# Keys of the second attention computed inside the last output product, two output tiles to a PSUM bank, and the bias added to x ahead of the last power

## The reference, cut to what matters

```
x = x + attention0(norm(x), ctx)          # 16 heads of 16, with biases bq, bk, bv, bo
x = x + ffn0(norm(x))                     # fp4-quantised, silu(gate) * up, width 704
x = x + attention1(norm(x), ctx, mask)    # 16 heads of 64: k = ctx @ W_K, v = ctx @ W_V
x = x + ffn1(norm(x))                     # width 1024
# ffn1: h = fix(x @ w1 + b1); h = fix(piecewise-linear gelu(h)); out = fix(h @ w2 + b2)
```

## Time and profile before

| what | value |
|---|---|
| median of 3 runs | 1011.18 us |
| their range | 1006.55 to 1011.65 us |
| the profiled execution | 1006.48 us |
| its span, first to last instruction | 1004.5 us |
| busy: PE, DVE, ACT, POOL | 913.8, 702.4, 599.6, 194.3 us |
| granted clock of PE, mean | 0.987 |
| chain that ended last | PE 55%, DVE 26%, ACT 10% |

### The profile page before, as it was taken

One profiled execution on the slowest core, in us unless ns is written; L12 is line 12 of the kernel. 1 busy time (PEld: TensorE's weight loads), 2 busy tenths in 40 slices (PEclk: granted clock), 3 DMA queues, 4 the chain that ended last, 5 costly groups with the idle time before them and its releaser, 6 DMA issues.

```text
span 1004.5 us, 16041 instructions
## 1 busy us (share of the span) xinstructions
PE 913.8 (91%) x5508; PEld 583.5 (58%) x5508; DVE 702.4 (70%) x2192; ACT 599.6 (60%) x1671; POOL 194.3 (19%) x307
## 2 busy tenths in 40 slices
PE   3888889999979999999979999999998999999985
PEld 1455565667555666566555556566755565656743
DVE  5799682674789786474697978267488978637358
ACT  2688433882679633794458943498166973369442
POOL 2000000782000000375100000078200000037300
PEclk8999999999999999999999999999999999999999
DMA  9400100000000010000000000000000000000000
GB/s 295 171 1 1 27 1 22 1 2 1 1 1 18 6 27 22 1 1 2 0 1 7 17 27 1 22 2 2 1 0 1 17 7 1 0 1 2 1 0 21
DMA packets 14943, 18.33 MB, mean 18 GB/s; under 512 B 3472, under 2 KB 12048, under 8 KB 14864
## 3 DMA queue, kind: packets, MB, share of 16 engines
q1 hardware_dynamic: 12800, 15.53, 4.8%
q10 hardware_dynamic: 2064, 1.78, 0.6%
HBM read 15.21 MB, written 2.10 MB: 17 GB/s over the span
## 4 chain that ended last, share of the span: by engine, by line
PE 55%; DVE 26%; ACT 10%; issue 4%; SPq 2%; DMA 1%; POOL 1%; POOLq 0%; DVEq 0%; ACTq 0%
PE bank L1030 22%; PE bank L1045 9%; PE bank L1216 5%; PE bank L1296 5%; PE bank L1194 4%; PE bank L1136 4%; DVE row_max L833 3%; ACT ring L564 3%; PE bank L1113 2%; ACT ring L504 2%; ACT ring L601 2%; SPq L391 1%; DVE act_s L755 1%; DMA w_s<-w 1%; DVE big_q L800 1%
## 5 line engine op out<-in xcount | busy, mean ns | idle before, releaser
L418 POOL TENSOR_TENSOR rstd<-var_eps,minus_half 128x2 f32<-128x2 f32 x32 | 22.7, 713 | 643.8 <-DVE var_eps L750 643.8
L504 ACT ACTIVATE ring<-bank 128x512 f32<-128x512 f32 x228 | 125.7, 605 | 28.4 <-PE bank L1045 28.3
L429 POOL TENSOR_TENSOR ring<-ring,row_inv 128x256 f32<-128x256 f32 x192 | 111.9, 612 | 98.7 <-DVE row_inv L927 98.7
L1045 PE MATMUL bank<-ident_s,ring 128*128 128x128 f32 x768 | 105.8, 281 | 4.2 <-ACT ring L504 2.6
L1045 PEld LDWEIGHTS bank<-ident_s,ring 128*128 128x128 f32 x768 | 83.7, 142 | 41.9 <-issue 19.2
L601 ACT ACTIVATE ring<-ring,row_max 128x256 f32<-128x256 f32 x192 | 95.4, 501 | 14.2 <-DVE row_max L920 13.8
L1030 PE MATMUL bank<-ctxT_s,wk_s 128*128 128x512 f32 x160 | 82.0, 639 | 19.9 <-DVE wk_s L992 7.2
L564 ACT ACTIVATE ring<-bank,row_max 128x256 f32<-128x256 f32 x192 | 88.3, 494 | 15.6 <-DVE row_max L833 15.5
L833 DVE TENSOR_REDUCE row_max<-bank 128x2 f32<-128x512 f32 x128 | 79.3, 681 | 16.1 <-PE bank L1113 15.4
L920 DVE CUSTOM_DVE_ANT_0 ring<-bank,maskbias 128x256 f32<-128x256 f32 x192 | 69.9, 420 | 19.2 <-issue 19.2
L1030 PE MATMUL bank<-wgu_s,act_s 128*128 128x352 f32 x256 | 78.8, 461 | 2.9 <-ACT act_s L498 2.9
(11 more groups left out here) (159 smaller groups left out, 1662.3 us busy)
## 6 DMA issues: line engine op xcount, KB each, us to landing
ctxT_s<-ctxT SPq DMA_DIRECT2D x4, 512.0 KB, 3.7
x_s<-x SPq DMA_DIRECT2D x4, 512.0 KB, 4.0
w_s<-w SPq DMA_DIRECT2D x2, 1024.0 KB, 15.7
out<-act_s SPq DMA_DIRECT2D x16, 128.0 KB, 1.7
wk_s<-wk SPq DMA_DIRECT2D x1, 1024.0 KB, 12.9
wv_s<-wv SPq DMA_DIRECT2D x1, 1024.0 KB, 13.9
wq_s<-wq SPq DMA_DIRECT2D x1, 1024.0 KB, 16.2
wo_s<-wo SPq DMA_DIRECT2D x1, 1024.0 KB, 18.0
```

The costliest lines, as they stand in the source:

```text
L429: ins = pool.tensor_tensor(probs1[i % PRING1][:, a, :], probs1[i % PRING1][:, a, :], row_inv[:, i, a:a + 1].to_broadcast([P, SEQ]), ALU.mult)
L504: act.activation(probsT[u % TRING][:, :, :].rearrange("p a q -> p (a q)"), psum(at, key)[:], ACT.Copy).then_inc(drain(at, key), 1)
L1045: ins = pe.transpose(psum(at, key)[:, c * SEQ + a * P:c * SEQ + (a + 1) * P], tile[:, a, c * P:(c + 1) * P], ident_s[:])
```

## The change

Four edits go together.

1. The first three key chunks k1(0), k1(1), k1(2) of a crossing move out of rounds 1 to 3 and into the output product. PE's order is now: output chunks 0 to 3, k1(0), chunk 4, k1(1), chunk 5, scores of round 0, chunks 6 and 7, k1(2). ACT drains k1(0) and k1(1) behind the last query drain, and k1(2) between the exponentials of units 1 and 2 of round 0. They go through banks 4, 5 and 5.
2. To free banks 4 and 5, the four output tiles share two banks (6 and 7), two tiles in each, and `output_bias` is two operations of 512 columns in place of four of 256. In a crossing it stands between the normalising of units 1 and 2 instead of ahead of unit 0.
3. k1 is kept in big_v and v1 in big_q, so the lower half of big_v is no longer a gelu buffer: `GELUS` is 4, and `hidden(m)` waits for yT(m - 4). The opening's raw weights and temporaries move from big_v to big_q with it.
4. POOL's `bias_x(g + 1)` stands ahead of the last `ln_power`, right behind the mask conversion.

The opening pass keeps its order; the closing pass gets edits 2 and 3.

```diff
-GELUS = 5
+GELUS = 4
+KEYS_AHEAD = 3
@@ jobs_layer0
     if with_last_layer:
         jobs_last_out(jobs)
+        for m in range(KEYS_AHEAD):
+            jobs.add(("k1", m), 4 + min(m, 1))
@@
-        jobs.add(("k1", r - 1), 7)
+        if not with_last_layer or r > KEYS_AHEAD:
+            jobs.add(("k1", r - 1), 7)
@@ jobs_last_out
-    for t in range(TILES):
-        jobs.add(("o2", t), 4 + t)
+    for h in range(HALVES):
+        jobs.add(("o2", h), 6 + h)
@@
-        q1, k1, c1 = big_k, big_q, big_c
-        v1 = big_v[:, :, :].rearrange("p (t n) c -> p t (n c)", t=TILES)
+        q1, k1, c1 = big_k, big_v, big_c
+        v1 = big_q[:, :, :].rearrange("p (t n) c -> p t (n c)", t=TILES)
-        gelu_buf = [... ((big_v, 0), (big_v, 1), (big_c, 0), (big_c, 1), (ring, 0))]
+        gelu_buf = [... ((big_v, 1), (big_c, 0), (big_c, 1), (ring, 0))]
@@ gpsimd
                 mask_to_bias()
+                bias_x(g + 1)
                 ln_power(g * 4 + 4)
-                bias_x(g + 1)
@@ scalar, last_layer
+                if with_layer0:
+                    for m in range(KEYS_AHEAD - 1):
+                        layer1_key(at, m)
@@ scalar, layer0_heads
-                        layer1_key(at, r - 1)
+                        if with_weights or r > KEYS_AHEAD:
+                            layer1_key(at, r - 1)
...
                         for i in round_units0(r):
+                            if r == 0 and i == 2 and not with_weights:
+                                layer1_key(at, KEYS_AHEAD - 1)
                             exponentials(i)
@@ vector, output_bias
-                for t in range(TILES):
-                    dve.wait_ge(*is_filled(at, ("o2", t)))
-                    dve.tensor_tensor(ffn_out[:, t, :], psum(at, ("o2", t))[:, 0:DM], b2_s[:], ALU.add)...
+                for h in range(HALVES):
+                    tiles = slice(2 * h, 2 * h + 2)
+                    dve.wait_ge(*is_filled(at, ("o2", h)))
+                    dve.tensor_tensor(ffn_out[:, tiles, :], psum(at, ("o2", h))[:].rearrange("p (t d) -> p t d", t=2),
+                                      b2_s[:].unsqueeze(1).to_broadcast([P, 2, DM]), ALU.add)...
@@ vector, layer0_heads
-                        else:
+                    for i in round_units0(r):
+                        if i == 2 and g is not None:
                             output_bias(at)
-                    for i in round_units0(r):
                         normalize(i)
@@ tensor, last_out
-                        key = ("o2", t)
-                        ins = pe.matmul(psum(at, key)[:, 0:DM], ..., start=(m == 0), stop=(m == FC1 - 1))
+                        key, n = ("o2", t // 2), t % 2
+                        ins = pe.matmul(psum(at, key)[:, n * DM:(n + 1) * DM], ...,
+                                        start=(m == 0 and n == 0), stop=(m == FC1 - 1 and n == 1))
@@ tensor, layer0_heads
-                    if r <= ROUNDS0:
+                    if r <= ROUNDS0 and (with_weights or r > KEYS_AHEAD):
                         layer1_key(at, r - 1)
@@ tensor, crossing
-                last_out(crossing_pass(g), g, range(FC1 - 1))
+                last_out(crossing_pass(g), g, range(4))
+                layer1_key(crossing_pass(g), 0)
+                last_out(crossing_pass(g), g, range(4, 5))
+                layer1_key(crossing_pass(g), 1)
+                last_out(crossing_pass(g), g, range(5, 6))
                 layer0_scores(crossing_pass(g), 0)
-                last_out(crossing_pass(g), g, range(FC1 - 1, FC1))
+                last_out(crossing_pass(g), g, range(6, FC1))
+                layer1_key(crossing_pass(g), 2)
```

More of the change, by code:

```diff
@@ L287, in xattn_ffn_twice @@
         yT = big_q
-        gelu_buf = [big[:, 4 * n:4 * n + 4, :] for big, n in ((big_v, 0), (big_v, 1), (big_c, 0), (big_c, 1), (ring, 0))]
+        gelu_buf = [big[:, 4 * n:4 * n + 4, :] for big, n in ((big_v, 1), (big_c, 0), (big_c, 1), (ring, 0))]
         xn0T = ring[:, 4:4 + KC, :]
@@ L299, in xattn_ffn_twice @@
                             for n in range(2))
-        down_raw = big_v[:, 0:3, :].rearrange("p a b -> p (a b)").rearrange("p (r k) -> p r k", r=KC)
+        down_raw = big_q[:, 0:3, :].rearrange("p a b -> p (a b)").rearrange("p (r k) -> p r k", r=KC)
         weight_pieces = [raw.rearrange("p r k -> p (r k)")[:, n:n + PIECE] for raw in (gate_raw, up_raw) for n in range(0, FC0 * DM, PIECE)]
         weight_pieces += [down_raw[:, r, 0:FF0] for r in range(KC)]
-        flat_v = big_v[:, :, :].rearrange("p a b -> p (a b)")
-        piece_temps = [flat_v[:, FC0 * DM + n * PIECE:FC0 * DM + (n + 1) * PIECE] for n in range(2)]
+        flat_q = big_q[:, :, :].rearrange("p a b -> p (a b)")
+        piece_temps = [flat_q[:, FC0 * DM + n * PIECE:FC0 * DM + (n + 1) * PIECE] for n in range(2)]
         keys_loaded, values_loaded, queries_loaded = sem("keys_loaded"), sem("values_loaded"), sem("queries_loaded")
@@ L526, in layer0_query, with layer1_key @@
                 ins.then_inc(drain(at, ("q0", c)), 1)
+            def layer1_key(at, m):
+                act.wait_ge(*is_filled(at, ("k1", m)))
+                act.activation(k1[:, m, :], psum(at, ("k1", m))[:], ACT.Copy).then_inc(drain(at, ("k1", m)), 1)
             def last_layer(at, g, with_layer0):
@@ L549, in layer0_inputs @@
                     evacuate_xT(at, 0, h, xn0T)
-            def layer1_key(at, m):
-                act.wait_ge(*is_filled(at, ("k1", m)))
-                act.activation(k1[:, m, :], psum(at, ("k1", m))[:], ACT.Copy).then_inc(drain(at, ("k1", m)), 1)
             def piece_steps(n):
@@ L802, in output_bias @@
             def output_bias(at):
-                for t in range(TILES):
-                    dve.wait_ge(*is_filled(at, ("o2", t)))
-                    dve.tensor_tensor(ffn_out[:, t, :], psum(at, ("o2", t))[:, 0:DM], b2_s[:], ALU.add).then_inc(drain(at, ("o2", t)), 1)
+                for h in range(HALVES):
+                    tiles = slice(2 * h, 2 * h + 2)
+                    dve.wait_ge(*is_filled(at, ("o2", h)))
+                    dve.tensor_tensor(ffn_out[:, tiles, :], psum(at, ("o2", h))[:].rearrange("p (t d) -> p t d", t=2),
+                                      b2_s[:].unsqueeze(1).to_broadcast([P, 2, DM]), ALU.add).then_inc(drain(at, ("o2", h)), 1)
             def finish_tile(at, g, t):
-                dve.wait_ge(*is_drained(at, ("o2", t)))
+                dve.wait_ge(*is_drained(at, ("o2", t // 2)))
                 dve.tensor_scalar(ffn_out[:, t, :], ffn_out[:, t, :], FIX, FIX, ALU.add, ALU.subtract).then_inc(o_round, 1)
@@ L1073, in last_out @@
                 if chunks[0] == 0:
-                    for t in range(TILES):
-                        wait_free(at, ("o2", t))
+                    for h in range(HALVES):
+                        wait_free(at, ("o2", h))
                 for m in chunks:
@@ L1078, in last_out @@
                     for t in range(TILES):
-                        key = ("o2", t)
-                        ins = pe.matmul(psum(at, key)[:, 0:DM], yT[:, m, t * P:(t + 1) * P], w2_s[:, m, :], start=(m == 0), stop=(m == FC1 - 1))
-                        if m == FC1 - 1:
+                        key, n = ("o2", t // 2), t % 2
+                        ins = pe.matmul(psum(at, key)[:, n * DM:(n + 1) * DM], yT[:, m, t * P:(t + 1) * P], w2_s[:, m, :],
+                                        start=(m == 0 and n == 0), stop=(m == FC1 - 1 and n == 1))
+                        if m == FC1 - 1 and n == 1:
                             ins.then_inc(fill(at, key), 1)
```

## The result

The changed kernel takes 1002.41 us (median of 6 runs, 1001.17 to 1003.85) against 1009.61 us for before (6 runs, 1006.55 to 1011.65). The ratio is 0.9929, 95% interval [0.9908, 0.9949]: 0.71% faster, and even the near end of the interval is just past the 0.5% that the prediction took for the least that a measurement tells. The forecast of 1007.0 us had the direction, and the range 999.5 to 1011.5 holds the result, but the likeliest outcome, no change, did not come. The gain is 7.2 us by the medians where the sum said 4.2. The two profiled executions show yet another number: spans of 1004.5 and 1000.9, 3.6 us apart.

What follows compares the result with a forecast made beforehand. DVE was taken to bound the output product, short waits the hand-over and PE the rounds. Three crossings of 0.25 + 1.25, less 0.3 in the closing pass, gave 4.2 us off the 1011.18 median: 1007.0, range 999.5 to 1011.5.

Steps and rivals of the forecast that it cites:

- the likeliest outcome, no change: Whole kernel: a time that the measurement cannot tell from before, within 0.5% or 5 us; chance 0.55.
- the sum: Whole kernel: three crossings of 0.25 + 1.25 = 1.5 are 4.5, less 0.3 in the closing pass: 4.2 us faster.
- all 2.05 of the blocking: DVE's two normalisings behind the last ln_power: bias_x on POOL costs DVE 2.05 us, of which 0.25 was taken as gain.
- its spare time: Output product, 268 to 286 us: DVE owns the path and PE has about 3.9 us to spare.
- PE's list: Output product with three keys: PE runs unbroken, k1(2) starts at 287.7 to 287.9, scores of round 1 gain 1.0.
- the round without its key: Round 1 to round 2 scores: 6.5 us against 6.7, bringing the gain per crossing from 1.0 to 1.25.
- no wait on ACT or more of the 2.05: Crossings: exponentials run through, or more of DVE's blocked time comes back; 999.5 to 1004.5 us, chance 0.18.
- The overrun: Output product: changing chunks cost 1.99, not 1.72; a crossing loses 1.3, 1015.4 in all; chance 0.06 full, 0.11 half.
- The new wait is not there: Round 0: k1(2) filled by 288.4, exponentials run through; 8.4 us gained, 1002.8; shares a chance of 0.18.
- Its price of the wait: Round 0: scores of round 1 come 2.4 earlier without ACT's wait for k1(2), against 1.0 with it.
- Starving: Gelu steps: four buffers leave DVE waiting 0.5 a step, 2 us a crossing, 6 in all: 1013; chance 0.03.

Runs made afterwards that it cites:

- both experiments: Two kernels: before with only bias_x moved ahead of the last ln_power, ratio 0.9987; the changed kernel with bias_x put back, ratio 0.9944.
- two keys ahead: Changed kernel with k1(2) returned to round 3, so only k1(0) and k1(1) are made in the output product: 997.93 us, ratio 0.9897.
- with the bias out of the way: Changed kernel with k1(2) back in round 3 and the output bias behind the normalising of all four units: 996.48 us, ratio 0.9894.
- the gap filled: Before with two output tiles a bank, plus an unread 128x512 product where PE idled ahead of k1(0): 1005.84 us, ratio 0.9965.

## Why the prediction was right or wrong

*Edit 4.* Right: 0.25 forecast, 0.33 to 0.35 measured, and `bias_x` cost nothing in its new place. Had all 2.05 of the blocking been on the path, the move would have brought 6 us; by the group lengths it brought 1.0, in both experiments. The rule of the Trainium skill (SBUF — State Buffer, section "SBUF: two separate sides") is about the blocking alone, and there the rows agree: the pair ended 0.47 behind `bias_x` (249.50 and 249.03 by the earlier trace rows; the prediction rounds it to 0.4).

*Edit 3.* Right: 0 forecast, 0.03 measured; PE's wait of 1.0 ahead of the second query was 0.86, taken from its spare time as laid out.

*Edit 1, PE's list.* Right to a tenth. Against the first hidden product, k1(2) was forecast at 287.7 to 287.9 less 250.95, so 36.8 to 37.0 later; it came 289.25 - 252.36 = 36.89 later. The scores of round 1 gained 0.88, where 1.0 was forecast, and 0.07 of the difference is a misreading: the chain counts a group of matmuls that follows another without a stop only from the other's end, 293.28, while in PE's timeline the scores of before start at 293.21:

```profile
293.21 1.15 PE L1113 MATMUL bank<-big_k 32*128 32x256 f32 x16
```

So they start 42.26 behind the first hidden product before (250.95) and 41.38 after (252.36).

*Edit 1, the round without its key.* Here a term was mis-sized. Forecast were 6.5 us from the scores of round 1 to those of round 2 where before took 6.71, so 0.25 more to gain; measured are 300.40 - 293.74 = 6.66, so 0.05 more. The chain of waits after:

```profile
298.43 1.84 ACT big_k L571 x8
300.27 0.14 issue
300.40 1.15 PE bank L1127 x16
...
310.83 0.34 DVE big_c L837
```

I had added 0.05 between ACT's last exponential and PE's scores; it is 0.14. And from the scores to the first exponential I had 2.67, by the start that is 0.07 late; it is 2.74 in both kernels. The over_sums of round 3 come 0.51 later than in before in an execution that was 1.75 late, so 1.24 earlier, of which 0.34 is edit 4's. The 1.25 forecast for edit 1 were thus 0.93 at the scores of round 2 and 0.90 here, and over the whole group 0.87 is left. So a crossing gained 0.34 + 0.87 = 1.21, where the sum had 1.5.

*Edit 2.* Right: hidden in the crossings, 0.3 in the closing pass as forecast.

*The sum and the median.* This is where the prediction failed. "The same 4.2 off that gives 1007.0": by work the kernel gained 3.3, less than the 4.2, and the medians moved by 7.2. I took the spread of before, 1006.55 to 1011.65, as something both kernels would share. In part it was a cost of the kernel: the clock fell behind the very idle time that the change removes, and the sum has no term for it. The trace of before had it in plain sight, as a k1(0) of 1.96 in crossing 1 and of 3.28 and 3.23 in the other two, but I priced all three crossings from the first one, and called the three alike where their groups take 237.19, 238.88 and 235.69. In four profiled executions with that idle time seven of the twelve crossings fell, 1.75 an execution, so an estimate of what the change gives back is 1.75 x 1.67 = 2.9. With the 3.3 that makes 6.2, against 6.9 by the means of the two times six runs (1009.25 and 1002.36) and 7.2 by their medians, whose interval reaches from 5.1 to 9.3. That the range held the result is in part luck: its lower part was meant for no wait on ACT or more of the 2.05, neither of which came in the changed kernel.

*The rivals.* The overrun did not come, since chunks of different form follow each other at 1.72. "The new wait is not there" was not how the change went, and that its 1002.8 lies 0.4 from the result is chance. Its price of the wait, 1.4 a crossing, is near what two keys ahead gave back, 1.45, but there the output bias took a part, and with the bias out of the way it was 235.91 - 234.07 = 1.84. Starving is refuted.

## What to carry to other kernels

Price every repetition of a seam from its own rows: twins that differed by 1.7 us here carried a cost that no sum from one of them could hold. And runs that fall in two clusters are a reason to look for such a seam. Where PE stands still ahead of long products, a product that nobody needs can be worth more than it costs; better still is useful work moved there, as here. And when work is moved into a gap, what counts is who waits for the last thing in it: two keys in the gap beat three by 1.45 us a crossing, and the same three with the last one made earlier by 1.17.

## What the runs showed of the hardware

I had not expected PE's clock to fall behind an idle time of 2 us, in a stretch whose other idle times are at most 1.54. Of twelve crossings with 1.9 to 2.05 us of idle time ahead of k1(0), those of before and of the three kernels with one edit alone, seven fell; of the 21 of the changed kernel, its repeat, the one with bias_x back and the four versions with the keys or the bias placed otherwise, whose longest single idle time there is at most 1.3 us, none did, nor any of the three with the gap filled, which keep the idle times of 1.54. A fall cost 1.67 us. Why one gap of 2.04 costs 1.7 us and its twin nothing stays open: no run varied the place of the gap alone.
